# A decoder layer on one core: query and key columns in another order, stacked keys with pairs innermost, and two parts of an FFN layer moved between two cross scores

## The reference

```python
x = layernorm(x + self_attention(x))            # 16 heads of 16, causal, with biases
x = layernorm(x + cross_attention(x, ctx))      # 16 heads of 64, 77 context tokens, no bias
x = layernorm(x + ffn(x))                       # [x,-x] 512 -> 1024 -> 1024 -> 256, weights +1/-1
```

## Time and profile before

| | |
|---|---|
| profiled execution, its span | 2341.51 us, 2339.8 us |
| PE busy | 2148.4 us (92%) |
| PEld, DVE, ACT, POOL busy | 1898.8, 1492.0, 1123.2, 688.9 us |
| mean clock of PE granted in the span | 0.971 of full speed |
| chain that ended last, by engine | PE 62%, DMA 11%, SPq 9%, DVE 8%, issue 5%, ACT 4%, POOL 1% |
| largest DMA share on that chain | k_bd<-p2t, 10% |
| DMA packets | 205157, of them 184307 under 2 KB |

### The profile page before, as it was taken

How to read it: one execution, slowest core, us unless ns; L and a number is a source line. 1 busy time by engine, 2 the same in 40 slices (tenths; PEclk the granted TensorE clock), 3 DMA queues, 4 the chain that set the end, 5 groups by cost and what they waited for, 6 DMA issues and landing times.

```text
span 2339.8 us, 54614 instructions
## 1 busy us (share of the span) xinstructions
PE 2148.4 (92%) x18572; PEld 1898.8 (81%) x18572; DVE 1492.0 (64%) x4548; ACT 1123.2 (48%) x2568; POOL 688.9 (29%) x847
## 2 busy tenths in 40 slices
PE   7998689999999999999999999999999999999997
PEld 6877578888888888888888888888888888888886
DVE  4454456766676666666666766666666666666664
ACT  5544344545444544445444445444544444554452
POOL 2000223233333333332333333323233333332331
PEclk9999799999999999999999999999999999999999
DMA  8997433323332333333233333333322332333310
GB/s 256 286 294 208 95 69 74 68 60 59 63 66 47 72 72 72 72 72 65 60 57 67 59 54 72 72 72 72 69 60 57 63 67 51 68 72 72 72 42 10
DMA packets 205157, 196.58 MB, mean 84 GB/s; under 512 B 50131, under 2 KB 184307, under 8 KB 205043
## 3 DMA queue, kind: packets, MB, share of 16 engines
q1 hardware_dynamic: 205108, 195.94, 38.3%
HBM read 69.37 MB, written 58.87 MB: 55 GB/s over the span
## 4 chain that ended last, share of the span: by engine, by line
PE 62%; DMA 11%; SPq 9%; DVE 8%; issue 5%; ACT 4%; POOL 1%; DVEq 0%; POOLq 0%; ACTq 0%
PE ps L1192 12%; DMA k_bd<-p2t 10%; PE ps L1374 9%; PE ps L1340 5%; PE ps L1268 3%; PE ps L1283 3%; SPq L359 3%; PE ps L1232 3%; PE ps L1233 3%; PE ps L1358 3%; PE ps L1243 3%; PE ps L1173 3%; PE ps L1244 2%; PE ps L1142 2%; PE ps L1257 2%
## 5 line engine op out<-in xcount | busy, mean ns | idle before, releaser
L1232 PE MATMUL ps<-r_h,w 128*128 128x256 f16 x2048 | 474.6, 279 | 2.1 <-DVE r_l L838 2.1
L1233 PE MATMUL ps<-r_l,w 128*128 128x256 f16 x2048 | 474.8, 279 | 0.0
L852 DVE CUSTOM_DVE_ANT_0 junk<-ps,causal 128x128 bf16<-128x128 f32 (+1 forms) x1024 | 330.4, 356 | 166.0 <-PE ps L1257 154.2
L512 POOL TENSOR_TENSOR p<-p2r,inv 128x308 f32<-128x308 f32 x256 | 200.1, 782 | 312.5 <-DVE inv L902 311.1
L498 POOL TENSOR_SCALAR_AFFINE_SELECT probs<-probs 128x512 f32<-128x512 f32 x256 | 163.4, 638 | 436.9 <-ACT probs L649 435.3
L624 ACT ACTIVATE p2r<-ps,low 128x77 f32<-128x77 f32 x1024 | 242.4, 341 | 43.9 <-DVE low L891 43.2
L649 ACT ACTIVATE probs<-ps 128x768 f32<-128x768 f32 x256 | 204.2, 812 | 84.1 <-PE ps L1268 83.8
L1374 PE MATMUL ps<-vo_h,p2t 128*128 128x256 f32 (+1 forms) x1280 | 239.7, 290 | 1.8 <-DVE p2t L909 1.8
L587 ACT ACTIVATE r_h<-ps 128x512 f16<-128x512 f32 x256 | 151.6, 592 | 176.2 <-PE ps L1233 153.4
L1232 PEld LDWEIGHTS ps<-r_h,w 128*128 128x128 f16 x2048 | 203.4, 99 | 39.1 <-issue 9.6
L522 POOL TENSOR_SCALAR var_eps<-mv 128x2 f32<-128x2 f32 x96 | 20.9, 217 | 697.8 <-DVE mv L827 697.8
(11 more groups left out here) (145 smaller groups left out, 4894.3 us busy)
## 6 DMA issues: line engine op xcount, KB each, us to landing
vo_scratch<-vo_out SPq DMA_DIRECT2D x80, 448.0 KB, 4.4
vo<-vo_scratch SPq DMA_DIRECT2D x64, 512.0 KB
q_st<-p2t SPq DMA_DIRECT2D x192, 128.0 KB
k_bd<-p2t SPq DMA_DIRECT2D x192, 128.0 KB, 6.6
q<-q SPq DMA_DIRECT2D x128, 128.0 KB, 2.1
k_bd<-k_scratch SPq DMA_DIRECT2D x64, 154.0 KB, 3.5
x_in<-in_x SPq DMA_DIRECT2D x32, 256.0 KB, 2.7
out<-y SPq DMA_DIRECT2D x32, 256.0 KB, 6.6
```

Source lines behind the costliest of these rows:

```text
L512: pool.tensor_tensor(unit_probs(t), raw, inv.unsqueeze(3).to_broadcast([P, TB, 2, SK]), ALU.mult)\
L852: dve.tensor_tensor_reduce(out=junk[:, e, b * P:b * P + width], in0=ps[:, bank + b, e * width:(e + 1) * width], in1=causal[:, (1 - b) * P: ...
L1232: pe.matmul(dst, w1[:, kk, m * P:(m + 1) * P], r0_h[:, kk, :], start=kk == 0, stop=False)
L1233: last = pe.matmul(dst, w1[:, kk, m * P:(m + 1) * P], r0_l[:, kk, :], start=False, stop=kk == KF - 1)
```

## The change

Two things are edited. First, the columns of a query or key chunk stand in another order: chunk m of the two holds the pairs 2n + m (n = 0 to 3) of both parities, row e * 64 + d * 4 + n. A stack transfer now reads 64 partitions (one parity) of both chunks, which lie next to each other, so that one source row has 2 KB, and writes two pairs next to each other; `k_bd` becomes `[partition, parity, pair, token]`, so that its rows are contiguous as those of `q_st` are. The 12 transfers keep their places in SP's queue, their waits, their 128 KB and their 16 destination partitions. The matmuls that read `k_bd` get the new indices. Second, on PE parts 18 and 19 of layer 1 go between `cross_scores(i, 6, f)` and `cross_scores(i, 7, f)`; the stretches behind become parts 20 and 21, and 22 and 23.

```diff
--- before.py
+++ after.py
@@ -90,7 +90,7 @@
 
 
         q_st = sb("q_st", [P, NP, S], F32R)
-        k_bd = sb("k_bd", [P, NP, 2, S], F32R)
+        k_bd = sb("k_bd", [P, 2, NP, S], F32R)
         v = sb("v", [P, TB, H, 2 * HD], F32)
         k2_bd = sb("k2_bd", [P, KX, 2 * SK], F32)
 
@@ -230,8 +230,8 @@
             pieces = [(stage_qkv[:, :, 2 * D:], dst[:, :, 2 * D:])]
             for kk in range(KD):
                 for m in range(2 * KD):
-                    src = stage_qkv[:, kk, (m // 2) * D:(m // 2 + 1) * D].rearrange("p (n e d) -> p e d n", e=2, d=HD)
-                    pieces.append((src[:, m % 2], dst[:, kk, m * P:(m + 1) * P].rearrange("p (d n) -> p d n", n=NP)))
+                    src = stage_qkv[:, kk, (m // 2) * D:(m // 2 + 1) * D].rearrange("p (n a e d) -> p a e d n", a=2, e=2, d=HD)
+                    pieces.append((src[:, m % 2], dst[:, kk, m * P:(m + 1) * P].rearrange("p (e d n) -> p e d n", e=2, d=HD)))
             return pieces
 
         def first_part(w, c):
@@ -340,27 +340,27 @@
                 sp.wait_ge(a_qk, nth(j, 4, 2))
                 sp.dma_start(q_st[ROW_M:64 + ROW_M + 1:64, :, :].bitcast(F32), zero_d).then_inc(q_stacked, 16)
                 for r in (0, HD):
-                    sp.dma_start(q_st[r:r + HD, :, :].bitcast(F32), qk_h[:, 0, :].bitcast(F32)).then_inc(q_stacked, 16)
+                    sp.dma_start(q_st[r:r + HD, :, :].bitcast(F32), qk_h[0:64, 0:2, :].bitcast(F32)).then_inc(q_stacked, 16)
 
             def query_stacks_end(j):
 
                 for r in (64, 64 + HD):
-                    sp.dma_start(q_st[r:r + HD, :, :].bitcast(F32), qk_h[:, 1, :].bitcast(F32)).then_inc(q_stacked, 16)
+                    sp.dma_start(q_st[r:r + HD, :, :].bitcast(F32), qk_h[64:P, 0:2, :].bitcast(F32)).then_inc(q_stacked, 16)
                 sp.wait_ge(d_qk, nth(j, 4, 2))
                 for e in range(2):
                     r = 64 * e + 2 * HD
-                    sp.dma_start(q_st[r:r + HD, :, :].bitcast(F32), qk_l[:, e, :].bitcast(F32)).then_inc(q_stacked, 16)
+                    sp.dma_start(q_st[r:r + HD, :, :].bitcast(F32), qk_l[64 * e:64 * e + 64, 0:2, :].bitcast(F32)).then_inc(q_stacked, 16)
 
             def key_stacks(j):
 
                 sp.wait_ge(a_qk, nth(j, 4, 4))
                 for e in range(2):
                     for r in (64 * e, 64 * e + 2 * HD):
-                        sp.dma_start(k_bd[r:r + HD, :, e, :].bitcast(F32), qk_h[:, KD + e, :].bitcast(F32)).then_inc(k_stacked, 16)
+                        sp.dma_start(k_bd[r:r + HD, e, :, :].bitcast(F32), qk_h[64 * e:64 * e + 64, KD:2 * KD, :].bitcast(F32)).then_inc(k_stacked, 16)
                 sp.wait_ge(d_qk, nth(j, 4, 4))
                 for e in range(2):
                     r = 64 * e + HD
-                    sp.dma_start(k_bd[r:r + HD, :, e, :].bitcast(F32), qk_l[:, KD + e, :].bitcast(F32)).then_inc(k_stacked, 16)
+                    sp.dma_start(k_bd[r:r + HD, e, :, :].bitcast(F32), qk_l[64 * e:64 * e + 64, KD:2 * KD, :].bitcast(F32)).then_inc(k_stacked, 16)
 
             def stack_max(j, half):
 
@@ -416,7 +416,7 @@
             for e in range(2):
                 sp.dma_start(stage_p[e::2], w_proj.rearrange("(k e p) n -> e p k n", e=2, p=64)[e]).then_inc(w_in[3], 16)
             for m in range(2 * KD):
-                src = b_qkv[(m // 2) * D:(m // 2 + 1) * D].rearrange("(p e d) -> e d p", e=2, d=HD)[m % 2]
+                src = b_qkv[(m // 2) * D:(m // 2 + 1) * D].rearrange("(n a e d) -> a e d n", a=2, e=2, d=HD)[m % 2]
                 sp.dma_start(bias_qk[:, m:m + 1], src, allow_slow_non_contiguous=True).then_inc(small_in, 16)
             sp.dma_start(bias_v[:], b_qkv[2 * D:3 * D].partition_broadcast(P)).then_inc(small_in, 16)
             for b in range(TB):
@@ -481,7 +481,7 @@
                                pattern=[[-1, P]], channel_multiplier=1).then_inc(const_pool, 1)
             pool.wait_ge(const_pool, 9)
             for e in range(2):
-                pool.memset(k_bd[64 * e + 32:64 * e + 64, :, e, :].bitcast(F32), 1.0).then_inc(const_pool, 1)
+                pool.memset(k_bd[64 * e + 32:64 * e + 64, e, :, :].bitcast(F32), 1.0).then_inc(const_pool, 1)
                 pool.wait_ge(const_pool, 10 + e)
             pool.wait_ge(small_in, 16 * 10)
 
@@ -1253,8 +1253,8 @@
 
                 if n >= 1:
                     pe.wait_ge(d_mx, nth(i, 2 * H, 4 * n))
-                pe.matmul(ps[:, bank, 0:2 * P], q_st[:, n, 0:P], k_bd[:, n, :, 0:P], start=True, stop=True)
-                pe.matmul(ps[:, bank + 1, :], q_st[:, n, P:S], k_bd[:, n, :, :], start=True, stop=True)\
+                pe.matmul(ps[:, bank, 0:2 * P], q_st[:, n, 0:P], k_bd[:, :, n, 0:P], start=True, stop=True)
+                pe.matmul(ps[:, bank + 1, :], q_st[:, n, P:S], k_bd[:, :, n, :], start=True, stop=True)\
                   .then_inc(pe_sq, 1)
 
             def scores_by_key(i, n):
@@ -1266,7 +1266,7 @@
                 for e in range(2):
                     for kb in (1, 0):
                         last = pe.matmul(ps[:, 4 + 2 * (n % 2) + e, (1 - kb) * S:(2 - kb) * S],
-                                         k_bd[:, n, e, kb * P:(kb + 1) * P], q_st[:, n, :], start=True, stop=True)
+                                         k_bd[:, e, n, kb * P:(kb + 1) * P], q_st[:, n, :], start=True, stop=True)
                 last.then_inc(pe_st, 1)
 
             def values(i, g):
@@ -1476,10 +1476,11 @@
                 cross_scores(i, 4, f)
                 cross_scores(i, 5, f)
                 cross_scores(i, 6, f)
+                layer1_until(f, Z_XT, 20)
                 cross_scores(i, 7, f)
                 cross_transposes(i, 0, 0)
                 cross_transposes(i, 0, 1)
-                layer1_until(f, Z_XT, 21)
+                layer1_until(f, 20, 22)
                 cross_output(i, 0, 0)
                 cross_transposes(i, 0, 2)
                 cross_output(i, 0, 1)
@@ -1487,7 +1488,7 @@
                 cross_transposes(i, 1, 0)
                 cross_transposes(i, 1, 1)
                 next_scores(4)
-                layer1_until(f, 21, 24)
+                layer1_until(f, 22, 24)
                 cross_output(i, 1, 0)
                 cross_transposes(i, 1, 2)
                 cross_output(i, 1, 1)
```

## The result

The changed kernel takes 2312.5 us (median of 4 runs, 2311.45 to 2313.18) against 2339.2 us before: a ratio of 0.9883, with a 95% interval of 0.9866 to 0.9900. That is faster by 1.2%, as forecast in its direction, and by 27 us instead of 14. The profiled execution of it has a span of 2309.7 us.

A forecast was written before the change was run, and what follows sets the result against it. PE, busy 92% of the span, was taken as the bound, leaving its idle time and low clock. 0 from part 1, 10.9 us from part 2 and 3.7 us of clock made 14.6 us: about 2326 us, range 2300 to 2362.

The forecast's parts named there:

- Part 2: Layer 1 parts moved ahead of the last cross scores on PE: saves 0.35 us an iteration, 10.9 us in 31.
- the pace of part 1: Stack transfers with new columns and 2 KB rows: a stack still passes every 1.13 us, so the gain is 0.
- The comparison that led to it: Stack backlog at 116 GB/s against value-output loads at 337, equal rows: only the number of destination partitions was said to differ.
- each 0.1 us of pace saves 1 us of wait: Clause on the stack backlog for cases between rows as the whole limit and no effect of rows.
- three signs of being wrong: Stack stretch above 130 or below 110 GB/s; line 1256's wait below 2 us; line 1374 taking over more than 0.5 us.
- The clock: Stretches at 1.2 instead of 2.4 GHz after the stacks' wait: three fewer, at 1.24 us each, save 3.7 us.
- near the edge of being followed by the low clock: Reading of PE's waits for the stacks: 2.22 and 2.35 us came before the fast iteration, 2.2 to 2.6 us overall.
- Rows as the whole limit: Rival: each packet has a price whatever its length, so the stack backlog goes; 114 us less, 2226 us; chance 0.09.
- Sources as the bound: Rival: reading 64 partitions makes a stack 10% slower, ten stacks 1.1 us later an iteration; 2364 us; chance 0.09.
- Part 2 gives nothing: Rival: `p2t` comes late and the wait only moves from line 1340 to 1374; 2340 us, no change; chance 0.16.
- The rule of the ports: For stack destinations: 16 neighbouring partitions reach 4 of 16 ports, about 109 GB/s, whatever the rows; 1.2 us a stack.

The follow-up runs named there:

- p2_only: Kernel before, with only the layer 1 parts moved on PE as in the change, columns and stacks as before: 2329.2 us, ratio 0.9959.
- the spread kernels: Three kernels whose stack transfers write 16 partitions two apart instead of 16 neighbours: 2225.1, 2216.5 and 2216.7 us.
- spread_before: Kernel before, but each stack transfer writes 16 partitions two apart; rows of 1 KB and layer 1 as before: 2225.1 us, ratio 0.9502.
- spread_after: Changed kernel, but each stack transfer writes 16 partitions two apart; rows of 2 KB stay: 2216.7 us, ratio 0.9475.
- rows1k: Changed kernel, but query and key chunks stored in turn, so each stack source row is cut into 1 KB rows: 2339.9 us, ratio 0.9997.
- kbd_only: Kernel before, with only the new `k_bd` layout, so key stacks have contiguous destinations: 2340.9 us, ratio 0.9998.
- p1_only: Changed kernel with layer 1 in its old place, so only the new columns and stacks: 2323.7 us, ratio 0.9926.

## Why the forecast came out as it did

**Part 2** came nearly as worked out. An iteration saves 0.40 us where 0.35 was taken, and p2_only gains 11.4 us where it was 10.9; but with two low stretches fewer, which the forecast has as a term of its own. By the waits alone it is 16.6 - 0.5 us at line 1340 less 6.2 us at line 1374, 9.9 us or 0.31 us an iteration, and the spread kernels, which have no low stretches there, show 0.31 us too.

**The failed step is the pace of part 1**: "I take no change, 1.13 us". The pace did change: by the means of 117 and 123 GB/s a stack of 131 KB passes every 1.12 us before and every 1.07 us after. Ten stacks then come about 0.5 us earlier by this rough rate; the last ones land 0.3 us sooner after their issue, and the wait was shortened by 0.38 us (0.34 without the first three). That is 12.0 us in the view of waits where 0 had been put, and with the low stretches that went along, part 1 gave 17 us by itself.

The comparison that led to it was right in its main point, and its conclusion too wide. The prediction says that the two stretches differ only in the number of destination partitions; the kernel shows one difference more, since the value outputs are loaded from a DRAM scratch and the stacks are copied inside SBUF. So that the destination makes the stretch slow was first shown by the spread kernels, which move the destinations alone: spread_before gains 117 us over the kernel before, with rows of 1 KB, and spread_after 96 us over the changed kernel, with rows of 2 KB. But this does not show that rows cost nothing *within* the slow stretch. There rows1k and the changed kernel differ by the rows alone, and by 27 us. The forecast weighed "rows are all" against "rows are nothing", and left the middle to one clause ("each 0.1 us of pace saves 1 us of wait"). By that price, a pace better by 0.04 us, or 4%, gives 0.4 us of wait and 12 us in 31 iterations: nearly all of the gain that was missed. None of the three signs of being wrong came up (122 GB/s lies between 110 and 130, the wait stayed above 2 us, line 1374 took far less than 0.5 us). They were set too wide to see it; only the share, 1.07 where over 1.1 was expected, and the wait, 2.1 where it was 2.2 to 2.6, fell outside what was to be seen.

**The clock** was a smaller miss. Three low stretches fewer were put down, 3.7 us; the traces have 23 of 27 before and 18 after, and five at 64.06 - 62.99 = 1.07 us are 5.4 us. With 12.0 us of the stacks' wait and 9.9 us of part 2 this makes 27 us, the gain of the medians (the two profiled executions are 30 us apart). A count from one trace is uncertain by two or so: kbd_only, with the wait and the time of the kernel before, has 21. That part 1 does lower it is borne out by all executions: their mean granted clock is 0.968 to 0.972 before, 0.970 to 0.972 in p2_only, 0.974 to 0.975 in the changed kernel and 0.974 to 0.978 in p1_only. The prediction's reading that a wait of this length stands near the edge of being followed by the low clock isn't shown. In the changed kernel the 27 waits are nearly alike (1.95 us once, else 2.08 to 2.14), and its iterations go low, low, full in a strict turn; before, four full iterations followed waits of 2.22, 2.35, 2.24 and 2.65 us, the last of them the longest of all 27. So the length of the wait doesn't decide by itself, and what does stays open.

**The rivals.** Rows as the whole limit: refuted, since rows of 2 KB leave 2.33 us of wait, and rows of 1 KB none when spread. Its price, 103 us for wait and clock without part 2, is near the 117 us of spread_before, since it priced the backlog's going, whatever takes it away; that it was to be the rows was wrong. Sources as the bound: what is left in rows1k, 0.27 us an iteration instead of the 1.1 taken, fits it at a quarter of its price, is shown by elimination only, and is outweighed by the rows. Part 2 gives nothing: refuted.

**The rule of the ports.** By the Trainium skill, "SBUF — State Buffer", section "Door 1: The DMA port swizzle", 16 neighbouring partitions reach 4 ports, about 109 GB/s, and by its formula 16 partitions two apart reach 8. The spread kernels agree, with 211 against 122 GB/s and the issue as their limit; but no kernel here tries another step, so that it is the ports, and not the wider spread as such, is the page's account and not shown by a run. Its figure for 4 ports, 109 GB/s, is below the 116 to 122 GB/s measured here over transfers that go to different ports in turn, and the rule has no term for the row's length, which counted here; the measurement decides.

Open is why, in a stretch limited by its destinations, rows of 2 KB pass 4 to 5% faster, and whether it is the 64 sources that make rows1k slower than the kernel before. No kernel here takes these apart further.

## What to carry to other kernels

Where DMA engines are full and move far less than elsewhere in the same trace, compare the stretches by what they have in common and what they have not before pricing an edit: rows were equal here, destinations (and the memory that was read) were not, and one changed slice of the destination (every second partition) gave more than four times the gain of the whole change. A secondary cost inside such a limit is still to be priced: ask what a pace better by a few per cent does to the wait, and not only what none and all of it would do. Where a wait is followed by a low clock in some iterations, price both, and count the low iterations in more than one execution.

## What had not been expected of the hardware

Sixteen destination partitions two apart take 211 GB/s and more, where sixteen neighbours take 116 to 122. With sixteen neighbours, rows of 2 KB instead of 1 KB took 0.65 us off a backlog of ten stacks; with partitions two apart their length made no difference to the time. Rows of 1 KB from 64 partitions, in another order of the columns, came 0.27 us later than from 128. Waits of one length, 2.1 us, were followed by the lower clock in 18 of 27 iterations, two of every three in turn; those of 2.2 to 2.65 us in the kernel before in 23; and those of 0.8 us (ahead of line 1201, in every iteration of the spread kernels) in none.
